# A selective scan in 16 states per section: when side work, kept sums and carried results are issued, and a last step sum on GpSimd

## What is computed

```python
dts_r, Bs, Cs = (x_dbl[:, :, :R], x_dbl[:, :, R:R + N], x_dbl[:, :, R + N:])
dts = jnp.einsum('bkrl,kdr->bkdl', dts_r, dt_proj_w)
dt = jax.nn.softplus(dts + dt_proj_b[None, :, :, None])
A = -jnp.exp(A_logs).reshape(K, d, N)
...
def step(h, inp):
    dt_l, u_l, B_l, C_l = inp
    dA = jnp.exp(dt_l[..., None] * A)
    h = h * dA + (dt_l * u_l)[..., None] * B_l[:, :, None, :]
    y = jnp.einsum('bkdn,bkn->bkd', h, C_l)
    return (h, y)
```

## Time and profile before

| what | value |
|---|---|
| median of 3 runs | 10391.0 us (10381.18 to 10395.99) |
| profiled execution | 10387.62 us, of which the span is 10385.7 us |
| busy over the span | PE 81%, DVE 67%, ACT 43%, POOL 41% |
| the four scans, start of the first scan instruction to the end of the last | 931.81, 932.49, 928.84 and 932.38 us |

### The profile page before, as it was taken

How to read it: one execution, slowest core, us unless ns; L and a number is a source line. 1 busy time by engine, 2 the same in 40 slices (tenths; PEclk the granted TensorE clock), 3 DMA queues, 4 the chain that set the end, 5 groups by cost and what they waited for, 6 DMA issues and landing times. The chain is left out here.

```text
span 10385.7 us, 129266 instructions
## 1 busy us (share of the span) xinstructions
PE 8379.6 (81%) x40748; PEld 6067.1 (58%) x40748; DVE 6946.5 (67%) x9145; ACT 4443.7 (43%) x8493; POOL 4258.6 (41%) x2945
## 2 busy tenths in 40 slices
PE   4777777777777777599999999967849899896657
PEld 2444444434443444389999999966625555554445
DVE  6999899989998999644444444443247566643446
ACT  4666566656665666422222222222423444453331
POOL 3999599959995999421111111100000000000001
PEclk8999999999998999899999999988968999998668
DMA  4555355535553555200000000013120100103000
GB/s 130 162 162 162 110 162 160 163 109 164 160 162 110 161 163 162 82 18 10 14 12 15 10 15 12 10 58 80 70 100 19 33 15 19 23 7 132 20 21 18
DMA packets 332597, 835.13 MB, mean 80 GB/s; under 512 B 35796, under 2 KB 111832, under 8 KB 318654
## 3 DMA queue, kind: packets, MB, share of 16 engines
q1 hardware_dynamic: 331910, 826.64, 25.9%
HBM read 758.85 MB, written 39.08 MB: 77 GB/s over the span
## 5 line engine op out<-in xcount | busy, mean ns | idle before, releaser
L754 POOL TENSOR_TENSOR ss_work<-ss_dtu,ss_ringb 128x768 f32<-128x768 f32 x1536 | 2758.0, 1820 | 252.2 <-POOLq L59 248.8
L618 PE MATMUL ss_ps<-ss_work,ss_ident 128*128 128x512 f32 (+1 forms) x6144 | 2278.7, 517 | 448.5 <-POOL ss_work L764 329.6
L618 PEld LDWEIGHTS ss_ps<-ss_work,ss_ident 128*128 128x128 f32 x6144 | 1222.5, 203 | 1224.4 <-issue 879.4
L738 DVE TENSOR_TENSOR_SCAN ss_work<-ss_ps,ss_last,ss_work 128x768 f32<-128x768 f32 x1024 | 1810.2, 1800 | 98.3 <-issue 44.3
L671 ACT ACTIVATE ss_ps<-ss_dt,ss_a_neg 128x768 f32<-128x768 f32 x1536 | 1376.1, 896 | 272.9 <-DVE ss_work L738 254.5
L1234 ACT ACTIVATE stu_XT<-cv_ps 128x384 fp32r<-128x384 f32 x768 | 377.8, 492 | 1788.9 <-DVE cv_ps L1281 1361.4
L723 DVE TENSOR_TENSOR ss_work<-ss_work,ss_ps 128x1152 f32<-128x1152 f32 x768 | 1018.5, 1326 | 1.2 <-ACT ss_ps L679 1.2
L2295 DVE TENSOR_REDUCE at_top<-at_ps 128x1 f32<-128x384 f32 x1512 | 727.5, 546 | 400.5 <-PE at_ps L2213 400.5
L2276 ACT ACTIVATE at_probs<-at_ps 128x768 f32<-128x768 f32 x864 | 653.6, 808 | 657.3 <-PE at_ps L2232 656.4
L738 DVE TENSOR_TENSOR_SCAN ss_work<-ss_ps,ss_work 128x768 f32<-128x768 f32 x512 | 879.2, 1743 | 66.9 <-POOL ss_work L754 36.3
L1275 DVE TENSOR_TENSOR stu_XT<-cv_ps,stu_XT 128x384 fp32r<-128x384 f32 x768 | 428.2, 558 | 637.9 <-ACT stu_XT L1234 615.1
(11 more groups left out here) (561 smaller groups left out, 14919.1 us busy)
## 6 DMA issues: line engine op xcount, KB each, us to landing
ss_ringb<-scan_rows SPq DMA_DIRECT2D x768, 384.0 KB, 3.7
ss_ringc<-scan_rows SPq DMA_DIRECT2D x768, 384.0 KB, 3.8
c_w<-in_l_ffn_w SPq DMA_DIRECT2D x52, 1024.0 KB, 13.3
at_packs<-at_high SPq DMA_DIRECT2D x64, 288.0 KB, 5.4
c_w_last<-in_l_ffn_w SPq DMA_DIRECT2D x12, 1024.0 KB, 13.5
cv_raw<-in_l_ffn_phi_odd SPq DMA_DIRECT2D x16, 576.5 KB, 3.6
cv_raw<-in_l_ffn_phi_even SPq DMA_DIRECT2D x16, 576.0 KB, 4.2
at_packs<-at_qk SPq DMA_DIRECT2D x32, 288.0 KB, 5.5
```

The costliest lines, as they stand in the source:

```text
L618: return pe.matmul(acc[:, d * WIN + a:d * WIN + e], ident[:, :], weighed[:, t % DEEP, d, a:e], start=n == 0 and e - a == 512, stop=n == NS ...
L738: dve.tensor_tensor_scan(hid[:, t % DEEP, d, ::step], decay[d][:, ::step], drive[:, t % DEEP, d, ::step], start, ALU.mult, ALU.add).then_i ...
L754: pool.tensor_tensor(drive[:, t % DEEP, d, :], dtu[:, t // NST % 2, d, :], ringb[:, t % RING, :], ALU.mult).then_inc(s["driven"], 1)
```

## The change

- The 6 input jobs move from states 3 to 8 to states 4 to 9, and exp, ln by one state. No job stands in state 3, so the special case in PE's state 0 goes; the job of state t + 2 now stands at the head of every state.
- Five sum jobs instead of six, in states 10 to 14. The last one (group 1, last 256 columns) becomes an addition in SBUF by POOL, behind its product of state 12. POOL's two input products are in states 11 and 13 (10 and 13 before). Who needs the second group's steps also waits for `sum_last`.
- The pieces of `y` are added in states 5 to 10 (three portions a group: the first piece, the two short ones, the last) instead of states 3 to 6 (two portions a group).
- The first increment of `summed` moves one matmul on, behind bank 1, and the copy of group 0 waits for it alone: it starts before the last 512 columns (bank 2) are summed.
- In column sections the copy runs over its elements in the other order: it writes `y` in runs of 16 neighbours and reads PSUM with a step of 48 elements, where before it read PSUM in order and wrote `y` with a step of 48.

```diff
-    INPUT_AT, SUM_AT = (3, 4, 5, 6, 7, 8), (9, 10, 11, 12, 13, 14)
+    INPUT_AT, SUM_AT = (4, 5, 6, 7, 8, 9), (10, 11, 12, 13, 14)
-    EXP_AT, LOG_AT, READY_AT = (5, 8), (6, 9), (10, 13)
-    FIRST_Y, KEEP_AT = 3, (1, 2)
+    EXP_AT, LOG_AT, READY_AT, SUM_LAST_AT = (6, 9), (7, 10), (11, 13), 12
+    FIRST_Y, KEEP_AT = 5, (1, 2)
...
-                if n != 1:
-                    beside(t + 2)
-                if 0 <= n - FIRST_Y < 2 * D2:
+                beside(t + 2)
+                if 0 <= n - FIRST_Y < 3 * D2:
+                    d, part = (n - FIRST_Y) // 3, (slice(0, 1), slice(1, 3), slice(3, 4))[(n - FIRST_Y) % 3]
...
                     add_weighed(t, 0, 0, 512)
-                    beside(t + 3)
...
-                add_weighed(t, 0, 512, WIN).then_inc(s["summed"], 1)
-                add_weighed(t, 1, 0, 256)
+                add_weighed(t, 0, 512, WIN)
+                add_weighed(t, 1, 0, 256).then_inc(s["summed"], 1)
...
             def keep_sums(i, d):
-                act.wait_ge(s["summed"], 2 * NST * (i + 1))
-                act.activation(window(y[:, d, :], SECTIONS[i]), acc[:, d * WIN:(d + 1) * WIN].rearrange("p (a b) -> p a b", b=48), ACT.Copy).then_inc(s["kept"], 1)
+                act.wait_ge(s["summed"], 2 * NST * (i + 1) - 1 + d)
+                order = "p a b -> p a b" if SECTIONS[i][0] % 2 == 0 else "p a b -> p b a"
+                total = acc[:, d * WIN:(d + 1) * WIN].rearrange("p (a b) -> p a b", b=48)
+                act.activation(window(y[:, d, :], SECTIONS[i]).rearrange(order), total.rearrange(order), ACT.Copy).then_inc(s["kept"], 1)
...
+                    if n == SUM_LAST_AT:
+                        pool.wait_ge(s["soft"], D2 * (i + 1) + 2)
+                        z = dt[:, (i + 1) % 2, 1, WIN - SIDE:WIN]
+                        pool.tensor_tensor(z, z, dtu[:, (i + 1) % 2, 1, WIN - SIDE:WIN], ALU.add).then_inc(s["sum_last"], 1)
```

More of the change, by code:

```diff
@@ L300, in selective_scan_mixer @@
         s1 = Signals(nc, "ss1", "loaded framed projected padded cleared conv_own conv_done convolved gated zed zgated made even_kept odd_kept")
-        s2 = Signals(nc, "ss2", "b0 b1 b2 b3 c0 c1 c2 c3 first_stored even_stored odd_stored kept_x copied driven decayed scanned weighted pool_weighted ended summed kept z_full z_kept exponent soft added dt_ready")
+        s2 = Signals(nc, "ss2", "b0 b1 b2 b3 c0 c1 c2 c3 first_stored even_stored odd_stored kept_x copied driven decayed scanned weighted pool_weighted ended summed kept z_full z_kept sum_last exponent soft added dt_ready")
         s3 = Signals(nc, "ss3", "mean centred squared varied logged sd_ready normed gated summed added stored")
@@ L621, in _ @@
                 i, n = t // NST, t % NST
-                if n != 1:
-                    beside(t + 2)
-                if 0 <= n - FIRST_Y < 2 * D2:
-                    d, half = (n - FIRST_Y) // 2, (n - FIRST_Y) % 2
-                    for a, e, rhs in list(pieces(y[:, d, :], SECTIONS[i], d))[2 * half:2 * half + 2]:
+                beside(t + 2)
+                if 0 <= n - FIRST_Y < 3 * D2:
+                    d, part = (n - FIRST_Y) // 3, (slice(0, 1), slice(1, 3), slice(3, 4))[(n - FIRST_Y) % 3]
+                    for a, e, rhs in list(pieces(y[:, d, :], SECTIONS[i], d))[part]:
                         pe.matmul(acc[:, a:e], ident[:, :], rhs, start=False, stop=False, skip_group_check=True)
```

10 lines of the change are left out of this document (8 added, 2 removed).

## The result

The changed kernel takes 10336.3 us, median of 5 runs, against 10391.0 before: a ratio of 0.9948 (95% interval 0.9932 to 0.9964), 54.7 us less. The forecast had 29.6 less, and its range ended 3.7 us above the result. The direction was right, the size was not.

What follows compares the result with a forecast made beforehand. POOL's own work was taken to bound sections 0 to 10. Additions +30.4, idle time -55 and last sections -5 gave -29.6: 10358 from the profiled 10387.6, or 10361 us as median, range 10340 to 10400.

Steps and rivals of the forecast that it cites:

- The bound: In the four scans, POOL's own work makes up nearly all of the time of sections 0 to 10.
- The idle time to be won: POOL's 65 us idle in sections 0 to 10 shrink to some 10; last sections lose 5 more.
- The addition: The last sum's 256 columns on POOL take 0.69 us each, a similar row less 0.05 overlap, without cover.
- the term +30.4: 44 POOL additions, 11 sections in 4 images, at 0.69 us each add 30.4 us, 27 to 33.
- the lowest case of the prediction's bounds: 10348 us for the whole kernel: each addition takes 0.61 us and no POOL idle time is left.
- The order step: At the section boundary, no job in state 3: PE's sums and the job of state 4 come 1.7 us sooner.
- The half clock: Rival: at the section boundary PE's lower clock slows state 1's sums by 2.7 us; 10379 us, chance 0.25.
- The slower copies: Rival: ACT's stepped PSUM reads at section ends cost more than the stepped writes did; 10425 us, chance 0.05.
- The stops that stay: Rival: DVE's stops before states 3 and 4 wait for something other than the jobs; 10421 us, chance 0.08.
- bound of 10 us: A long piece of y beside state 10's sum job exceeds by 0.5 us: up to 10 in 20 column sections.
- stops in states 10 to 14: Sign against the forecast: DVE stopping in these states of a section would show it wrong; no size given.

Runs made afterwards that it cites:

- two_additions: The changed kernel with a second POOL addition of 256 columns in state 12, its result unused: 10360.6 us.
- one_column: The changed kernel with POOL's addition cut to 1 of 256 columns, the rest of that sum left undone: 10312.7 us.
- copy_and_bank: The kernel before with only the new order of the copies and the copy of group 0 started a bank sooner: 10341.2 us.
- before_warm: The kernel before with 12 zero matmuls a section on PE, around the sums of states 14, 15 and 0: 10336.4 us.
- copy_bank_job1: copy_and_bank with the job of state 3 moved to the head of PE's state 1; six sum jobs, no POOL addition: 10323.7 us.
- table_alone: The changed kernel with its new job states and POOL addition, but old order and start of the copies and y in its old states: 10375.7 us.
- copy_bank_split592: copy_and_bank with 592 instead of 576 columns of the product on DVE, the rest on POOL: 10368.7 us.

## Why the prediction was right in direction and wrong in size

**The bound.** Right for the changed kernel (two_additions, one_column), where POOL's own work sets sections 0 to 10. In the kernel before it did so only from state 11 of a section to state 3 of the next. From state 4 or 6 on POOL had caught up: in image 2 it waits some 0.1 to 0.2 us before 49 of the 60 products of states 5 to 10 in sections 1 to 10, and moves at DVE's pace there, which the first failed step below takes up.

**The idle time to be won.** Right, and nearly to the us: counted 55 in sections 0 to 10 and 5 in the last ones, 60 in all; it was 61.4 and 3.4, 64.9 with the rounding. No stop in state 3, small ones in state 4 (up to 0.79 in sections 1 to 10) and no wait of POOL in state 4 came as written. The kernel before had such waits of 1 us or more in 23 of the 44 sections.

**The addition.** Its row was the right one: 0.742 us an instruction against 0.738 in the earlier trace rows, less 0.05 for the overlap, times 44: the 30.4 of the forecast.

**What failed, first: the term +30.4 as the whole rise of POOL's work, with its other work taken as fixed.** With +30.4 for the addition its busy time should rise by 30.4; it rose by 18.5. The prediction treated a state of POOL as one number and looked at 4.50 only as its pace. Two stretches of one state of the kernel before, the first where POOL is behind, the second where it has caught up and waits for DVE (POOL's busy time is the fifth):

```profile
1535.88:1540.38 4.50, 4.34 (x7) 2.53 (x8) 4.50 (x4) 2.50 (x6) 4.50 (x5) 0.50 0.67 175
1569.71:1574.39 4.68, 4.38 (x16) 2.52 (x15) 4.68 (x4) 3.85 (x10) 4.55 (x5) 1.00 0.48 169
```

The three instructions of a state overlap by about 0.05 us at each joint. Where one waits, a joint is lost and the busy time is 4.55. In the four scans the kernel before has a wait at 288 joints between POOL's instructions and the changed one at 48. 240 joints of 0.05 are 12 us, and 12 of the 30.4 came back: removing a wait of 0.13 gives the wait and the overlap. Kernels with no addition on POOL agree within 2 us with this count: copy_and_bank has 192 such joints (4.8 by the count) and 6.0 less busy time than the kernel before, before_warm 152 (6.8) and 5.5, copy_bank_job1 107 (9.0) and 10.2. No run changes the joints alone.

**What failed, second: the path behind the last scan.** The prediction took the copies as something at boundaries between sections. Each image ends with two copies that nothing covers, and its sum has no term for them: 7.7 us in four images, missed whole. A faster copy and an earlier start count there at full price.

**The sum again.** -64.9 of idle time, +18.5 of work and -7.7 at the ends of the images are -54.1; the medians differ by 54.7. From the forecast of -29.6 to there it is -5 (idle time), -12 (POOL's work) and -7.7 (ends of the images). The last two alone carry the result below the lowest case of the prediction's bounds, 10348.

**The order step had the wrong reason for its size.** The 1.7 us for the absent job was 3.1 in section 4; the six sum matmuls at the higher clock (3.6 to 1.89) give about the rest. It changed the time little, because POOL's work was already reached as the floor. But the working held alone would have failed: table_alone, the step by itself, gave 12.1 us by the median and 21.6 in the scans of the 37 that it should.

**The rivals.** The half clock went the other way. The prediction said that the sums of state 0 keep PE at work as long as today; in fact they ran at 1.2 GHz before and mostly at 2.4 GHz now. What PE did before them was shorter rests: 3.20 us before the job in the earlier trace rows, 1.09 and 0.96 now. The sums of states 14 and 15 stay slow (7.85), as before (8.14). Less work on PE at this place did not lower the clock. That the job had held PE at rest, waiting for the decay of its state, fits copy_bank_job1: with the job out of state 0 the slow sums fall from 40 to 15 (copy_and_bank against it). The absent job alone is not enough (table_alone, 40). The slower copies are out: 0.79 to 0.81 us for all, a step of 48 elements in PSUM costs ACT nothing, where the same step in its write to SBUF cost 0.7. The Trainium skill (SBUF — State Buffer, Specifications (TRN2)) gives SBUF lines of 16 bytes, with a penalty for each crossing to a new line, and PSUM lines of 8. The SBUF half agrees with these copies, 1.45 to 1.51 before and 0.80 now; for PSUM read by ACT no run here shows one. The stops that stay are out too: those before states 3 and 4 went from 7.1 and 22.5 to 0 and 3.6 an image.

**Added waits.** The new stop at state 0 (0.43 here), and small ones of 0.13 to 0.66 before state 13 in column sections, whose sum job stands on PE behind the last long piece of `y`, add up with the others to 4.6 us an image, 18.4 in all. The prediction's bound of 10 us was for the stops that the pieces of `y` bring: those before state 13 are 5.6 us in all. For the stop at state 0 it had no term. As POOL's work sets the time they cost nothing now. The prediction named stops in states 10 to 14 as a sign that it is wrong; they came, but the lag of POOL covered them.

## What to carry to other kernels

If one engine's own work makes up nearly all of the time, a better order can win little more than its idle time, and that can be read beforehand (65 us here, with 12 of regained overlap on top). Once it is won, only less work on that engine helps, and moving work off it before that can cost (copy_bank_split592). Try the small edits by themselves before a new table: two at the copies gave nearly as much as the whole. And look for the last iteration, where what is covered elsewhere lies open.
